# Head of an attention and mixture-of-experts kernel: order of block 0's projection, turns and rotations changed

## What is computed

```python
qkv = hidden_states @ Wqkv
q, k, v = jnp.split(qkv, 3, axis=-1)
q = rmsnorm(q, q_norm_w)            # x * rsqrt(mean(x*x) + 1e-6) * w
k = rmsnorm(k, k_norm_w)
q, k, v = (t.reshape(b, s, 16, 32) for t in (q, k, v))
q = rope(q, cos, sin)               # concat(x1*cos - x2*sin, x2*cos + x1*sin)
k = rope(k, cos, sin)
mask = (q_idx >= k_idx) & (q_idx - k_idx <= 255)
scores = jnp.einsum('bqhd,bkhd->bhqk', q, k) / sqrt(32)
probs = jax.nn.softmax(where(mask, scores, -inf), axis=-1)
o = jnp.einsum('bhqk,bkhd->bqhd', probs, v).reshape(b, s, h) @ Wo
x = layernorm(x + o)
```

## Time and profile before

| | |
|---|---|
| median of three runs | 1082.62 us |
| the profiled execution | 1083.18 us |
| its span, first to last instruction | 1081.4 us |
| PE busy | 1037.9 us, 96% of the span |
| DVE, ACT, POOL busy | 770.8, 637.2, 443.8 us |
| mean granted clock of PE | 0.98 of full |

### The profile page before, as it was taken

One profiled execution on the slowest core, in us unless ns is written; L12 is line 12 of the kernel. 1 busy time (PEld: TensorE's weight loads), 2 busy tenths in 40 slices (PEclk: granted clock), 3 DMA queues, 4 the chain that ended last, 5 costly groups with the idle time before them and its releaser, 6 DMA issues.

```text
span 1081.4 us, 19776 instructions
## 1 busy us (share of the span) xinstructions
PE 1037.9 (96%) x7120; PEld 852.8 (79%) x7120; DVE 770.8 (71%) x1146; ACT 637.2 (59%) x1303; POOL 443.8 (41%) x544
## 2 busy tenths in 40 slices
PE   6899999999999977999999999999999999999995
PEld 3677777777777754887888888888888888887884
DVE  6678888888888874866676767777666777674573
ACT  4466666666666554325667666666756666664353
POOL 2678888788888730000222222222222222311271
PEclk9899999999999996999999999999999999999998
DMA  5111111111111014448899999999999999985552
GB/s 187 39 36 32 42 33 32 34 51 32 42 32 32 23 38 136 137 146 277 221 267 258 260 266 261 251 260 275 252 275 240 279 261 263 259 231 132 165 197 87
DMA packets 120981, 171.36 MB, mean 158 GB/s; under 512 B 10114, under 2 KB 63746, under 8 KB 120804
## 3 DMA queue, kind: packets, MB, share of 16 engines
q1 hardware_dynamic: 111856, 149.54, 43.4%
q0 software_dynamic: 8736, 20.45, 11.6%
q10 hardware_dynamic: 292, 0.10, 0.0%
HBM read 151.45 MB, written 23.07 MB: 161 GB/s over the span
## 4 chain that ended last, share of the span: by engine, by line
PE 58%; DVE 1%; ACT 1%; issue 0%; DMA 0%; POOL 0%; ACTq 0%; POOLq 0%; DVEq 0%
PE up_ps L1407 4%; PE up_ps L1408 4%; PE up_ps L1406 4%; PE gate_ps L1406 4%; PE gate_ps L1407 4%; PE gate_ps L1408 4%; PE down_ps L1433 3%; PE down_ps L1432 3%; PE down_ps L1431 3%; PE e_up_ps L1457 3%; PE e_up_ps L1458 2%; PE e_up_ps L1459 2%; PE e_gate_ps L1466 2%; PE e_up_ps L1468 2%; PE e_up_ps L1466 2%; PE e_up_ps L1467 2%
## 5 line engine op out<-in xcount | busy, mean ns | idle before, releaser
L950 POOL DMA_INDIRECT sum_dram<-rows,target_i x39 | 62.7, 1608 | 365.2 <-ACT rows L1050 365.2
L1278 DVE TENSOR_TENSOR e_lo<-e_raw,e_hi 128x1408 fp32r<-128x1408 f32 x78 | 126.5, 1623 | 48.2 <-ACT e_hi L1024 48.2
L1024 ACT CAST e_hi<-e_raw 128x1408 fp32r<-128x1408 f32 x78 | 107.5, 1380 | 54.5 <-PE e_up_ps L1468 54.5
L317 ACT ACTIVATE prob<-score_ps,nbias 128x256 f32<-128x256 f32 (+1 forms) x256 | 117.8, 470 | 3.2 <-DVE nbias L439 3.2
L257 POOL TENSOR_TENSOR probT<-probT,masks 128x256 f32<-128x256 f32 x128 | 91.6, 742 | 58.9 <-DVE probT L469 58.9
L1283 DVE TENSOR_TENSOR ed_lo<-ed_raw,ed_hi 128x1024 fp32r<-128x1024 f32 x39 | 47.8, 1225 | 71.7 <-ACT ed_hi L1032 71.5
L956 POOL DMA_INDIRECT rows<-x_dram,token_i x39 | 52.8, 1353 | 100.0 <-DVE target_i L1247 70.7
L439 DVE TENSOR_REDUCE nbias<-score_ps 128x2 f32<-128x512 f32 (+1 forms) x128 | 86.3, 674 | 4.4
L324 ACT COPY probT<-probT_ps 128x512 f32<-128x512 f32 x64 | 37.6, 587 | 87.5 <-PE probT_ps L579 87.5
L545 PE MATMUL proj_ps<-wqkv_lo,xT_hi 128*128 128x512 f32 x180 | 79.3, 441 | 0.0
L547 PE MATMUL proj_ps<-wqkv_hi,xT_lo 128*128 128x512 f32 x180 | 71.9, 400 | 0.0
(11 more groups left out here) (243 smaller groups left out, 2985.3 us busy)
## 6 DMA issues: line engine op xcount, KB each, us to landing
e_raw<-in_We_gu SPq DMA_DIRECT2D x78, 704.0 KB, 6.2
ed_raw<-in_We_down SPq DMA_DIRECT2D x39, 512.0 KB, 5.3
raw_ring<-in_Ws_gu SPq DMA_DIRECT2D x58, 256.0 KB, 6.2
wd_raw<-in_Ws_down SPq DMA_DIRECT2D x44, 256.0 KB, 6.8
gu_raw<-in_Ws_gu SPq DMA_DIRECT2D x30, 256.0 KB, 6.1
ed_raw<-in_We_down SPq DMA_DIRECT2D x39, 192.0 KB, 6.7
xT_in<-in_xT SPq DMA_DIRECT2D x16, 256.0 KB, 2.8
x_in<-in_x SPq DMA_DIRECT2D x16, 256.0 KB, 3.2
```

The costliest lines, as they stand in the source:

```text
L317: nc.scalar.activation(prob[:, g % 2, h, seen], score_ps[:, h, seen], ACT.Exp, bias=nbias[:, s % 2, head:head + 1], scale=1.0, accum_out=r ...
L1024: nc.scalar.copy(e_hi[:, half * HK:(half + 1) * HK, :], raw_half(i, half)).then_inc(e_hi_made, 1)
L1278: nc.vector.tensor_tensor(e_lo[:, part, :], raw_half(i, half), e_hi[:, part, :].bitcast(FP32), ALU.subtract).then_inc(e_lo_made, 1)
```

## The change

It has these parts.

- On ACT, `split_xT(1)`, which waits for a DMA, moves from between the square of q and the scaling of the cosines to behind `take_q(0)`. `take_v(0)` moves from before `take_q(0)` to behind `take_k(0)`.
- On PE, the projection of the values of block 0 moves from group 1 to group 2 of step -1, behind the turn of q.
- The turn of k of block 0 writes `probT_ps[1]` instead of `probT_ps[0]`, and no longer waits for `lower_q(0)`. What reads it follows (`keys_ps`).
- On POOL, `v_difference(0)` also waits for the rotated k of block 0.
- The rotation of q of block 1 moves from POOL to DVE, into group 1 of step 0, between the second quarter of Wo and the weighing of k.

```diff
@@ -120,6 +120,10 @@
+        def keys_ps(a):
+            return turned_ps if a else probT_ps[1]
@@ v_difference, POOL @@
                 wait(pool, v_made, s + 1)
+                if s == 0:
+                    wait(pool, k_rot, 1)
@@ steps of POOL @@
                     if a:
                         scale_trig(pool, nc.gpsimd, a, 0, q_rms, q_cs)
+                    if a > 1:
                         wait(pool, k_rot, a)
                         rotate_cos(pool, nc.gpsimd, a, 0, rot_a[:, :], q_cs, q_weighted, q_part)
                         rotate_sin(pool, nc.gpsimd, a, 0, rot_a[:, :], rot_b[:, :], q_part, q_rot)
@@ take_k, ACT; lower_k on DVE reads keys_ps(a) in the same way @@
-                nc.scalar.copy(kT_hi[:, :, key_slot(a % RING), :], tiled(turned_ps[:, 0, :])).then_inc(kT_hi_made, 1)
+                nc.scalar.copy(kT_hi[:, :, key_slot(a % RING), :], tiled(keys_ps(a)[:, 0, :])).then_inc(kT_hi_made, 1)
@@ steps of ACT @@
                 if g == 2 and has(a):
                     take_q(a)
+                    if a == 0:
+                        split_xT(1)
                 if g == 3 and has(a):
                     take_k(a)
+                    if a == 0:
+                        take_v(0)
...
                     if s == -1:
-                        split_xT(1)
                         first_trig(0, q_rms, q_cs)
...
                         first_trig(1, k_rms, k_cs)
-                        take_v(0)
@@ steps of DVE @@
+                if g == 1 and a == 1:
+                    rotate_cos(dve, nc.vector, 1, 0, res[:, :], q_cs, q_weighted, q_part)
+                    rotate_sin(dve, nc.vector, 1, 0, res[:, :], oT[:, :], q_part, q_rot)
                 if g == 1 and has(a):
                     weigh(a, 1, kw_b, k_mm, k_weighted)
@@ turned_taken, PE @@
                 elif g == 2:
-                    wait(pe, qT_lo_made, min(s + 2, NB))
+                    if s >= 0:
+                        wait(pe, qT_lo_made, min(s + 2, NB))
@@ steps of PE @@
-                    turned(qk[:, 1, :]).then_inc(kT_mm, 1)
+                    turned(qk[:, 1, :], keys_ps(a)).then_inc(kT_mm, 1)
                 if part:
                     project(*part, range(KT) if first else range(KT // 2, KT), first).then_inc(done, 1)
-                if first and g == 1:
+                if first and g == 2:
                     project(x_hi, x_lo, wqkv_hi, wqkv_lo, 2, range(KT), True).then_inc(v_mm, 1)
```

More of the change, by code:

```diff
@@ L462, in lower_k @@
                 slot = key_slot(a % RING)
-                nc.vector.tensor_tensor(kT_lo[:, :, slot, :], tiled(turned_ps[:, 0, :]), kT_hi[:, :, slot, :].bitcast(FP32), ALU.subtract).then_inc(kT_lo_made, 1)
+                nc.vector.tensor_tensor(kT_lo[:, :, slot, :], tiled(keys_ps(a)[:, 0, :]), kT_hi[:, :, slot, :].bitcast(FP32), ALU.subtract).then_inc(kT_lo_made, 1)
             def probT_out(n):
@@ L548, in project, with turned @@
                 return last
-            def turned(src):
+            def turned(src, out=turned_ps):
                 for k in range(KT):
-                    last = nc.tensor.transpose(turned_ps[:, 0, k * P:(k + 1) * P], src[:, k * P:(k + 1) * P], ident[:, :])
+                    last = nc.tensor.transpose(out[:, 0, k * P:(k + 1) * P], src[:, k * P:(k + 1) * P], ident[:, :])
                 return last
```

## The result

Six executions of the changed kernel took 1073.72 us in the median (1072.93 to 1078.10), against 1082.53 us for the kernel before (six as well). The ratio is 0.9926, 95% interval 0.9907 to 0.9946. The forecast was 1074.5 us. The profiled execution took 1072.93 us, its span 1071.1 us.

What follows compares the result with a forecast made beforehand. PE was taken as the bound, with only the first 60 us able to change. The terms 3.1 + 1.9 + 3.1 = 8.1 us took 1083.18 to 1075.1, against the median 1074.5 us; range 1071.5 to 1078.8.

Steps and rivals of the forecast that it cites:

- a rival with a chance of 0.08: Behind 400 us: shifted clock falls in the hand-over cost or give 2 us or so; 1077 to 1079, chance 0.08.
- A: Head up to the first scores of block 0: they start at 24.85 instead of 27.99, gain 3.1 us.
- B: First scores to scores of group 1: full clock instead of half, gain 1.9 us; bounds nothing or all.
- the rival of the short holes: Head: holes of 1.6 and 1.4 us suffice for half clock; 1076.2, or gain 4 to 5 and 1078; chance 0.24.
- C: Block 1, rotation of q on DVE: turn of k 1.0 us earlier despite a 2.1 us hole; bounds 0 to 1.6.
- D: Behind the turn of k of block 1: clock holds, gain 2.1 us; bounds 0 to 2.8.
- the first rival: The rival of the short holes: half clock despite shorter holes, gain 6.4 or 4 to 5 us; chance 0.24.
- The slow rival: PE at half clock from the first hole until block 1: 5.7 us slower, 1088.3; chance 0.04.

Runs made afterwards that it cites:

- after_again: The changed kernel as it is, run a second time on one chip with three other kernels; 1075.9 us, ratio 0.9933 to the kernel before.
- xT_back: Changed kernel, but the split of x of block 1 stands ahead of the scaling of q's cosines on ACT again; 1078.1 us, ratio 0.9952.
- bank_back: Changed kernel, but the turn of k of block 0 writes the same bank as q's again and waits for DVE's subtraction; 1078.4 us, ratio 0.9950.
- vdiff_free: Changed kernel without the wait of v_difference(0) for the rotated k; 1076.7 us, ratio 0.9942.
- before_fill: Kernel before, with matmuls nobody reads, twelve and ten, before the turns of k of blocks 0 and 1; 1084.3 us, ratio 1.0006.
- wo_late: Changed kernel, but DVE splits the second quarter of Wo behind the weighing of k of block 1; 1076.0 us, ratio 0.9928.
- after: The changed kernel in its first run; median 1073.7 us, ratio 0.9926 to the kernel before, profiled execution 1072.93 us.
- v_split: Changed kernel, but the values' projection of block 0 is cut in two, six matmuls in group 1 and six behind the turn of q; 1077.3 us, ratio 0.9960.
- v_early: Changed kernel, but the values' projection of block 0 is back in group 1, ahead of the turn of q; 1077.0 us, ratio 0.9951.
- combo: Changed kernel with six q matmuls ahead of first scores, Wo's second quarter later, and block 0's values' projection cut about q's turn; 1075.6 us, ratio 0.9931.

## Why the prediction was right

- *PE bounds, and the first 60 us decide.* Right for the path: marker to end is the same work in all. But the end moves by some 5 us (1021.3 to 1026.8), mostly with the clock between 385 and 440 us, and the prediction had priced that at 2 us, as a rival with a chance of 0.08, where it is part of every run.
- *A, 3.1 us.* Measured by first square to first scores: 12.68 before, 9.66 in after_again (3.0) and 11.54 in the first run (1.1), where the clock fell 0.8 us into the values' projection. Roughly, of the 3.0 us the split of x behind the scaling brings 1.0 to 1.3 (xT_back), k's first product 1.0 (1.69 to 0.69 us), the other bank 0.3 to 0.7 (bank_back), and the turn of k at full clock 0.5. The step that was wrong inside it is the sentence that the new wait puts `v_step` behind the rotation: without the wait `v_step` is there as well, and the wait is idle (vdiff_free).
- *B, 1.9 us.* 1.81 to 1.82. That holes of 1.6 and 1.4 us don't bring half clock held in one trace of the change and not in the other, where the first hole was 1.92 us; the price was not B but 1.5 us within A (from the turn of q to that of k 4.81 us instead of 3.27). So the rival of the short holes comes and goes with the execution of one and the same kernel. When it came, 5.9 us of gain were left at the marker, where the rival had given 4 to 5.
- *C, 1.0 us.* 0.80: 14.68 instead of 15.48 us. The hole that the rotation makes is 1.70 us, not 2.1, and PE then finds 0.55 us more before the turn.
- *D, 2.1 us.* From turn to marker 7.13 and 7.10 us, so 2.14 and 2.17. The clock alone gives 2.47 (before_fill), 0.3 more: in the change PE waits less for `own_part` but 0.94 us for `lower_k`, which ends at 46.29 + 0.68 = 46.97, behind the last quarter of Wo.

```profile
46.29 0.68 DVE L472 TENSOR_TENSOR kT_lo<-probT_ps,kT_hi 128x512 fp32r<-128x512 f32 x1
```

- *Sum.* First square to marker: 7.8 us at full clock, 5.9 with one stretch at half, 8.1 forecast. The medians give 8.8 and 7.6. That the first of them lies within 0.8 us of the forecast is in part luck: single executions of the change lie 5 us apart and more. What bears the forecast out are its four terms in the rows. Two of its sums are off without harm: with C and D at their bounds the gain is 3.1 + 1.9 + 1.6 + 2.8 = 9.4 us and not 10, and the first rival gives 8.1 - 1.6 = 6.5 and not 6.4.
- *The slow rival.* No run was near it; no stretch at half in a head was longer than before's.

## What to carry to other kernels

Where PE waits, read the granted clock behind the wait: here some 4 us of the 8 were the clock (0.5 in A, 1.8 in B, about 2.1 in D) and only the rest the shorter chain. Before giving a move the credit, ask which one of several edits ends the wait last. Here the order on ACT and a rotation moved between engines did the work, while the moved projection, the other bank and the extra wait brought 0, 0.3 to 0.7 and 0 us. And compare heads by a marker within the trace: the end of a run carries the clock of all the later waits with it.

## What was not expected of the hardware

The same kernel had its stretches at half clock in different places from one execution to the next: a hole of 1.58 us was followed by full clock (after_again), one of 1.80 as well (wo_late), and one of 1.92 by half from 20.5 (after). Behind two holes of 1.13 and 1.45 us v_split fell to half at 25.5, and behind the same two v_early (1.12 and 1.45) did not. Behind holes of 0.55, 0.19 and 0.94 us wo_late fell at 45.5, and combo (0.55, 0.18 and 0.94) did not. A busy PE fell too: in after_again it is busy from 419.6 to 426.2 for the whole stretch and at 0.50, with the fall during 32 matmuls of 9 columns (416.62 to 420.70). It is so in twelve of the fourteen traces, but in the first of the change and in bank_back the same matmuls were followed by full clock until 440. What decides it, these runs leave open. The price is seen: the executions of one kernel and chip lie 3 to 8 us apart, in the main in step with their mean granted clock.
